# Modulation rows of layers 1 and 2 as two output rows, spread to the partitions by DMA

## What is computed

```python
for layer in (0, 1, 2):                      # layer 0: four experts, gated; layers 1 and 2: one MLP
    mod = silu(c) @ w_ada + b_ada            # [2, 864], one row for each batch element
    sh_msa, sc_msa, g_msa, sh_mlp, sc_mlp, g_mlp = split(mod, 6)
    x = x + g_msa * attention(ln(x) * (1 + sc_msa) + sh_msa)
    x = x + g_mlp * mlp_or_experts(ln(x) * (1 + sc_mlp) + sh_mlp)
x = x + ((x @ U) @ R - x @ U) @ U.T          # U from a QR of P, R from a matrix exponential of c
```

## Time and profile before

| | us |
|---|---|
| three executions: lowest, median, highest | 1153.31, 1158.83, 1162.43 |
| span of the profiled execution, first to last instruction | 1173.7 |
| PE busy, share of the span | 948.9, 81% |
| DVE busy, share of the span | 713.6, 61% |
| ACT busy, share of the span | 412.4, 35% |
| POOL busy, share of the span | 198.5, 17% |
| mean granted clock of TensorE (1 is 2.4 GHz, 0.5 is 1.2 GHz) | 0.638 |

### The profile page before, as it was taken

One profiled execution on the slowest core, in us unless ns is written; L12 is line 12 of the kernel. 1 busy time (PEld: TensorE's weight loads), 2 busy tenths in 40 slices (PEclk: granted clock), 3 DMA queues, 4 the chain that ended last, 5 costly groups with the idle time before them and its releaser, 6 DMA issues.

```text
span 1173.7 us, 12067 instructions
## 1 busy us (share of the span) xinstructions
PE 948.9 (81%) x3791; PEld 513.7 (44%) x3791; DVE 713.6 (61%) x2140; ACT 412.4 (35%) x742; POOL 198.5 (17%) x350
## 2 busy tenths in 40 slices
PE   4666889877898768889877788778887978989847
PEld 1432443335765433357644434535433534335326
DVE  4388767775353887772457767656677365564333
ACT  0302342324341333343424432415332436435412
POOL 5201014010240110042420000311002211012020
PEclk9999755556775655566866555657555656558556
DMA  3000001010111000001110000100000100000000
GB/s 101 13 1 10 16 6 43 1 29 1 29 29 29 17 1 1 1 16 42 34 38 0 1 1 1 29 1 1 1 1 0 30 0 1 1 1 1 6 5 11
DMA packets 22025, 16.01 MB, mean 14 GB/s; under 512 B 6427, under 2 KB 19391, under 8 KB 21962
## 3 DMA queue, kind: packets, MB, share of 16 engines
q1 hardware_dynamic: 21914, 15.22, 4.8%
q10 hardware_dynamic: 48, 0.02, 0.0%
HBM read 14.62 MB, written 0.61 MB: 13 GB/s over the span
## 4 chain that ended last, share of the span: by engine, by line
PE 61%; DVE 29%; issue 4%; ACT 4%; POOL 2%; DMA 0%; DVEq 0%; SPq 0%; ACTq 0%; POOLq 0%
PE o_bank L1289 11%; PE m_bank L1268 11%; DVE row_max L823 7%; PE s_bank L1257 3%; PE m_bank L1466 3%; PE d_bank L1350 3%; PE d_bank L1407 2%; PE d_bank L1409 2%; PE d_bank L1408 2%; PE m_bank L1276 2%; PE d_bank L1306 2%; PE d_bank L1307 2%; PE d_bank L1239 2%; PE d_bank L1392 2%; PE d_bank L1321 2%
## 5 line engine op out<-in xcount | busy, mean ns | idle before, releaser
L663 ACT ACTIVATE probs<-s_bank 128x512 f32<-128x512 f32 x384 | 220.4, 596 | 546.6 <-PE s_bank L1257 544.0
L823 DVE TENSOR_REDUCE row_max<-m_bank 128x1 fp32r<-128x512 f32 x384 | 256.0, 686 | 151.9 <-PE m_bank L1268 147.1
L1268 PE MATMUL m_bank<-k_t,q_t 32*128 32x512 f32 x384 | 216.5, 752 | 61.9 <-DVE q_rows L1079 24.2
L1257 PE MATMUL s_bank<-q_t,k_t 32*128 32x512 f32 x384 | 239.4, 749 | 5.8 <-ACT probs L663 4.9
L1289 PE MATMUL o_bank<-probs,v_aug 128*32 128x512 f32 x768 | 178.2, 1019 | 3.9 <-DVE o_tok L841 3.2
L1268 PEld LDWEIGHTS m_bank<-k_t,q_t 32*128 32x128 f32 x384 | 81.6, 271 | 181.9 <-issue 62.9
L1257 PEld LDWEIGHTS s_bank<-q_t,k_t 32*128 32x128 f32 x384 | 90.6, 272 | 30.9 <-ACT probs L663 16.1
L589 POOL TENSOR_TENSOR h_tok<-h_tok,mod 128x144 f32<-128x144 f32 x48 | 24.0, 499 | 297.3 <-DVE h_tok L882 297.3
L1407 PE MATMUL d_bank<-ff_hi,g_hi 128*128 128x144 f32 x192 | 60.7, 316 | 1.5 <-ACT g_hi L733 1.4
L1409 PE MATMUL d_bank<-ff_lo,g_hi 128*128 128x144 f32 x192 | 60.7, 316 | 0.0
L1408 PE MATMUL d_bank<-ff_hi,g_lo 128*128 128x144 f32 x192 | 60.5, 315 | 0.0
(11 more groups left out here) (232 smaller groups left out, 1639.4 us busy)
## 6 DMA issues: line engine op xcount, KB each, us to landing
raw_a<-in_L_cond_w_dram SPq DMA_DIRECT2D x20, 288.0 KB
raw_a<-in_L_cond_W_fc_dram SPq DMA_DIRECT2D x4, 288.0 KB
w_rows<-in_L_cond_W_dram SPq DMA_DIRECT2D x8, 141.8 KB
raw_d<-in_L_cond_w_dram SPq DMA_DIRECT2D x30, 36.0 KB
raw_a<-in_L_cond_w_dram SPq DMA_DIRECT2D x20, 36.0 KB
x_tok<-in_x_dram SPq DMA_DIRECT2D x2, 288.0 KB, 4.2
out_dram<-moe SPq DMA_DIRECT2D x4, 144.0 KB, 1.9
raw_d<-in_L_cond_w_dram SPq DMA_DIRECT2D x30, 4.0 KB
```

The source lines that it names most:

```text
L663: act.activation(probs[:, n % PROBS, :], s_banks[n % S_BANKS][:, :], ACT.Exp, scale=HD ** -0.5)\
L823: dve.tensor_reduce(row_max[:, grp % 2, t, MAXROW + 32 * j:MAXROW + 32 * j + 1], bk[:, :], AX.X, ALU.max).then_inc(drained, 1)
L1257: pe.matmul(s_banks[n % S_BANKS][:, :], k_t[rows, par, g, kt * P:(kt + 1) * P], q_t[rows, par, g, :], start=True, stop=True).then_inc(s["s ...
L1268: pe.matmul(bk[:, :], q_t[rows, par, g, t * P:(t + 1) * P], k_t[rows, par, g, :], start=True, stop=True).then_inc(s["max_full"], 1)
```

## The change

For layers 1 and 2 the four stages `mods` become two stages `rows(l)` and two stages `spread(l)`. `rows(1)` stands in block 0 where `mods(1, 0)` stood, `rows(2)` in block 2 where `mods(2, 0)` stood; `mods(1, 1)` and `mods(2, 1)` are gone. In `rows(l)` PE multiplies one column of silu(c) for each element, so the product has two output rows, one for each element. ACT copies the two halves out of PSUM into two rows of `g_raw` (borrowed from the MLPs) and stores them to a DRAM scratch tensor. `spread(l)`, at the start of block 1 for layer 1 and of block 3 for layer 2, reads each row back to 128 partitions, by two DMAs that ACT issues. DVE takes no part, but waits for the two transfers before the first normalisation of the layer.

The 1 of the scale now comes out of the product, in layer 0 too: `ada_d` has one more row, 1 for the two scale vectors and 0 for the others, set by POOL at the start, and `c_wide_d` has one more row of ones. So DVE's two instructions for each half in layer 0 become one copy of 432 columns. The first load of `ada_d` waits for that row.

```diff
     if block == 0:
-        out += [("norm", 1, "msa"), ("qkv", 1), ("prep", 1), ("prep", 2), ("mods", 1, 0), ("prep", 3)]
+        out += [("norm", 1, "msa"), ("qkv", 1), ("prep", 1), ("prep", 2), ("rows", 1), ("prep", 3)]
+    if block == 1:
+        out += [("spread", 1)]
     if block >= 1:
         out += after_attention(block - 1)
-    if block == 1:
-        out += [("mods", 1, 1)]
     if block == 2:
-        out += [("mods", 2, 0), ("prep", LAYER_ITEM[2])]
-    if block == 3:
-        out += [("mods", 2, 1)]
+        out += [("rows", 2), ("prep", LAYER_ITEM[2])]
     if 1 <= block < BLOCKS - 1:
         out += [("norm", block + 1, "msa"), ("qkv", block + 1)]
+    if block == 2:
+        out += [("spread", 2)]
...
+        mod_row = g_raw[0:B, :, :].rearrange("p i n -> p (i n)")[:, 0:6 * C]
...
             def load_ada(l):
                 if l:
-                    sp.wait_ge(s["mods_part"], 4 * l)
+                    sp.wait_ge(s["mods_full"], 4 if l == 1 else 6)
+                else:
+                    sp.wait_ge(s["ada_zeroed"], 1)
...
+            link(pool.memset(ada_d[:, :], 0.0))
+            pool.memset(ada_d[:, :].rearrange("p (h v c) -> p h v c", h=2, v=3)[:, :, 1, :], 1.0)\
+                .then_inc(s["ada_zeroed"], 1)
             pool.memset(raw_d[:, :], 0.0).then_inc(s["zeroed"], 1)
...
+            def rows(l):
+                copied = []
+                if seen.n.get("up_full", 0):
+                    act.wait_ge(s["g_lo_ready"], seen.n["up_full"])
+                for half in range(2):
+                    bk, drained, before = ring.take()
+                    act.wait_ge(s["mods_full"], 3 + 2 * l + half)
+                    act.activation(mod_row[:, 3 * C * half:3 * C * (half + 1)], bk[0:B, 0:3 * C], ACT.Copy)\
+                        .then_inc(drained, 1)
+                    copied.append((drained, before + 1))
+                for w in copied:
+                    act.wait_ge(*w)
+                act.dma_start(mod_scratch[l - 1], mod_row[:, :]).then_inc(rows_stored, 16)
+                yield
+
+            def spread(l):
+                act.wait_ge(rows_stored, 16 * l)
+                for b in range(B):
+                    act.dma_start(mod[:, b, l % 2, :, :].rearrange("p v c -> p (v c)"),
+                                  mod_scratch[l - 1][b:b + 1, :].to_broadcast([P, 6 * C])).then_inc(mods_in, 16)
...
-                    dve.tensor_copy(dst[:, 0:3:2, :], src[:, 0:3:2, :]).then_inc(s["mods_part"], 1)
-                    dve.tensor_scalar(dst[:, 1, :], src[:, 1, :], 1.0, None, ALU.add).then_inc(drained, 1)
+                    dve.tensor_copy(mod[:, b, l % 2, 3 * half:3 * half + 3, :],
+                                    bk[:, 0:3 * C].rearrange("p (v c) -> p v c", v=3)).then_inc(drained, 1)
...
             def norm(blk, kind):
                 b = blk % B
+                if kind == "msa" and blk >= B:
+                    dve.wait_ge(mods_in, 16 * B * (blk // B))
...
+            def rows(l):
+                for half in range(2):
+                    bk, _ = take(ring)
+                    pe.wait_ge(ada_in, 48 * (l + 1))
+                    cols = slice(3 * C * half, 3 * C * (half + 1))
+                    pe.matmul(bk[0:B, 0:3 * C], c_wide_a[:, :, 0], ada_a[:, cols], start=True, stop=False)
+                    pe.matmul(bk[0:B, 0:3 * C], c_wide_d[:, :, 0], ada_d[:, cols], start=False, stop=True)\
+                        .then_inc(s["mods_full"], 1)
+                yield
```

More of the change, by code:

```diff
@@ L120 @@
 WOVEN = [st for block in range(BLOCKS) for st in stages(block)]
-BANKS_OF = {"prep": (), "mods": (2,), "norm": (0, 2, 0), "qkv": (2, 2, 2, 2, 2, 2), "proj": (2,), "gate": (1, 0),
+BANKS_OF = {"prep": (), "mods": (2,), "rows": (2,), "spread": (), "norm": (0, 2, 0), "qkv": (2, 2, 2, 2, 2, 2), "proj": (2,), "gate": (1, 0),
             "mlp": (7, 0), "rotate": (2,)}
-ROOM = {"prep": (), "mods": (1,), "norm": (4, 1, 2), "qkv": (2, 2, 2, 2, 2, 2), "proj": (2,), "gate": (2, 1),
+ROOM = {"prep": (), "mods": (1,), "rows": (1,), "spread": (), "norm": (4, 1, 2), "qkv": (2, 2, 2, 2, 2, 2), "proj": (2,), "gate": (2, 1),
         "mlp": (1, 1), "rotate": (1,)}
@@ L258, in build @@
         ada_a = sb("ada_a", [P, 6 * C])
-        ada_d = sb("ada_d", [CR + 1, 6 * C])
+        ada_d = sb("ada_d", [CR + 2, 6 * C])
         c_a = sb("c_a", [P, B])
@@ L265, in build @@
         c_wide_a = sb("c_wide_a", [P, B, P])
-        c_wide_d = sb("c_wide_d", [CR + 1, B, P])
+        c_wide_d = sb("c_wide_d", [CR + 2, B, P])
         raw_a = sb("raw_a", [P, NM])
@@ L337, in build @@
         m_d = sb("m_d", [DW, B, C], F32R)
+        mod_scratch = nc.dram_tensor("mod_scratch", [2, B, 6 * C], F32, kind="Internal").ap()
         v_scratch = nc.dram_tensor("v_scratch", [B * VT, VP], F32, kind="Internal").ap()
@@ L357, in build @@
         scratch_in = sem("scratch_in")
+        rows_stored = sem("rows_stored")
+        mods_in = sem("mods_in")
         skew_in = sem("skew_in")
         y_stored = [sem(f"y_stored{i}") for i in range(2)]
-        names = ("zeroed ident_ready consts_ready weights_ready c_exp c_wide mods_part mods_full xn_ready "
+        names = ("zeroed ident_ready consts_ready weights_ready c_exp c_wide ada_zeroed mods_full xn_ready "
                  "h_tok_ready h_turned h_hi_ready qkv_full qk_normed hi_ready stack_ready stack_turned scores_full probs_ready "
@@ L668, in o_copy @@
                 act.activation(o_t[:, :], o_bank[:, :], ACT.Copy).then_inc(s["o_copied"], 1)
+            def rows(l):
[17 more added lines that the diff above has]
+                                  mod_scratch[l - 1][b:b + 1, :].to_broadcast([P, 6 * C])).then_inc(mods_in, 16)
+                return
+                yield
             def norm(blk, kind):
@@ L747, in solver @@
                     act.activation(q_rows[:, :], bk[0:S, 0:C], ACT.Copy).then_inc(drained, 1)
-            walk = {"norm": norm, "qkv": qkv, "gate": gate, "mlp": mlp}
+            walk = {"rows": rows, "spread": spread, "norm": norm, "qkv": qkv, "gate": gate, "mlp": mlp}
             def side(todo):
@@ L1504, in solver @@
                 last[chain] = ready
-            walk = {"mods": mods, "norm": norm, "qkv": qkv, "proj": proj, "gate": gate, "mlp": mlp,
+            walk = {"mods": mods, "rows": rows, "norm": norm, "qkv": qkv, "proj": proj, "gate": gate, "mlp": mlp,
                     "rotate": rotate}
```

3 lines of the change are left out of this document (removed).

## The result

The changed kernel takes 1162.49 us (median of 20 executions, 1152.71 to 1174.61), beside 1160.7 us for the kernel before in the same comparison (20 executions, 1142.96 to 1169.87). The ratio of the means is 1.0034 [1.0005, 1.0065]: no gain, and at most 0.65% slower. Forecast were 1147 us in 1136 to 1160. The ratios from here on, too, are of the means of all executions, each against before on the same chip, with 95% intervals from resampling and without three lone executions of experiments, at 1213 to 1257 us. Taken only over the executions within 1.5% of each kernel's fastest, a ratio is 0.5 to 1.2% higher (the change 1.0081 [1.0046, 1.0115], e1 1.0017, e8 0.9955), because that drops over half of before's, which spread over 2 to 3%, and few of the others'.

What follows compares the result with a forecast made beforehand. The prediction took PE and DVE to bound the kernel by turns (61% and 29% of the chain). Its terms, -6.4 - 3.5 - 0.4 - 1.3 = -11.6 us from 1158.8, gave 1147 us, range 1136 to 1160.

Steps and rivals of the forecast that it cites:

- Stages dropped, 6.4 + 3.5 us: Dropping modulation stages saves 6.4 us in block 3 (bounds 5.0 to 7.8) and 3.5 in block 1 (2.5 to 4.8).
- The turn of the maxima in block 1, +1.3: Block 1: DVE must wait at L830 for PE's turning of the maxima, 1.12 us and some 0.2 of signals.
- `rows`: Blocks 0 and 2: stationary operand of 2 columns instead of 128 saves 0.6 us a stage (bounds nothing to 2.5).
- DVE's copies, -0.7 in block 0: Blocks 0 and 2: DVE no longer copies the modulation products, saving 0.7 us each.
- ACT's hold-up, +0.9 in block 0: ACT's copy and store issue ahead of the exponential delay block 0's scores by 0.9 us; hidden in block 2.
- `spread`, nothing: Starts of blocks 1 and 3: ACT's two transfers cost nothing, hidden in idle time; without that cover, +0.7 us each.
- the order of slots: Block 3: up to 1.4 us of the saving might go because MLP and normalisation are each one step off.
- within 1%: Outcome class: measured time within 1% (11.6 us) of the kernel before, chance 0.49.
- Given back: Rival: PE only waits for DVE anyway, so just DVE's copies are saved, 2.8 us; 1156 us, chance 0.2.
- ACT pays: Rival: ACT's hold-up falls on the chain in block 2 and at both spreads, +2.3 us; 1150 us, chance 0.1.
- The clock: Rival: MLPs of blocks 1 and 3 change clock steps; worse 1171 us, chance 0.06; better 1136 us, chance 0.1.

Runs made afterwards that it cites:

- e1: The change with an empty slot where each dropped stage stood (blocks 1 and 3), so other stages keep their old steps: 1151.5 us, ratio 0.9930 to before.
- e8: e1 plus GpSimd splitting the next MLP's weights only after the present MLP's last g_lo: 1141.0 us, ratio 0.9833 to before.
- e7: The kernel before with the layer 1 and 2 modulation stages of the second batch element left out, empty slots instead: 1149.5 us, ratio 0.9895.
- e5: The change with block 1's solver parts at steps 21, 23, 26 moved one step on: 1162.4 us, ratio 1.0014 to before.
- e10: The change with the edits of e5 and e6 together: 1151.4 us, ratio 0.9916 to before.
- e13: The change with e6's later weight split and block 1's four MLPs at old steps 20, 22, 24, 26: 1140.4 us, ratio 0.9838 to before.
- e6: The change with GpSimd splitting the next MLP's weights only after the present MLP's last g_lo: 1150.9 us, ratio 0.9910 to before.
- e9: The kernel before with only GpSimd's weight split held until the present MLP's last g_lo: 1150.7 us, ratio 0.9923 to before.

## Why the prediction was wrong

**The sum agrees with the runs at the old places, though not term by term.** *Stages dropped, 6.4 + 3.5 us:* e7 has 12 us less than before by its ratio (8 to 16), and e1, which stands for the whole sum of 11.6, 8 to 10 less. No run separates the two blocks' terms. *The turn of the maxima in block 1, +1.3:* it came onto the chain as said. In the timeline DVE waits for it right behind the solver's step:

```profile
379.15 0.69 DVE L864 SCALAR_TENSOR_TENSOR q_t<-m_bank,q_t 128x512 fp32r<-128x512 f32 x1 [1.27 <-PE m_bank L1309]
```

*`rows`:* PE's stage in block 0 runs from 187.63 to 193.75 in the chain, 6.1 us against the 7.0 of the earlier trace rows. I took 0.6 us for the smaller loads; it is 0.85. By the estimate from the Trainium skill ("TensorE: Matmul & The Clock Gate", "LDWEIGHTS (loading the stationary operand)") it was 0.84, and the trace agrees in that sum, though not in the loads' own times, 311 and 83 ns. *DVE's copies, -0.7 in block 0:* they gave nothing beyond that. From the first product to the row maximum the chain takes 6.9 us, against 7.8 before (to 194.75 in the earlier trace rows), since DVE now waits for the scores that PE does behind the stage. The changed kernel:

```profile
187.63 1.53 PE d_bank L1350 x2
...
194.57 1.29 DVE row_max L857 x2
```

and the start of the stage before:

```profile
186.96 1.74 PE d_bank L1306 x2
```

*ACT's hold-up, +0.9 in block 0:* the second copy and the store lie ahead of the exponential as forecast. ACT's timeline in block 0, and PE's next scores:

```profile
193.78 0.52 ACT L687 ACTIVATE g_raw<-d_bank 2x432 f32<-2x432 f32 x1 [2.54 <-PE d_bank L1351]
194.39 0.46 ACTq L692 DMA_DIRECT2D mod_scratch<-g_raw  x1
194.96 1.09 ACT L672 ACTIVATE probs<-s_bank 128x512 f32<-128x512 f32 x2 [0.65 <-PE s_bank L1290]
...
195.60 0.79 PE L1290 MATMUL s_bank<-q_t,k_t 32*128 32x512 f32 x1 [0.46 <-ACT probs L672]
```

The 0.65 us in brackets hold the issue of the store, 0.46. The scores ended near 194.5, so the exponential came some 0.4 us late, and PE's next scores waited 0.46 for it. It cost nothing on the chain that ended last, which runs through DVE's row maxima there.

*`spread`, nothing:* issued at 235.88 and 4.2 us in landing by the page's DMA issues, where I took 13 for two; DVE needs it only near 370, and no wait for it shows.

```profile
mod<-mod_scratch ACTq DMA_DIRECT2D x4, 432.0 KB, 4.2
```

**The step that failed** is the one on the order of slots. In block 3 I allowed "1.4 us" for it ("the MLP and the normalisation are each one step off"), and only as a bound; in block 1, where three of the four MLPs moved (I counted all four), the sum has no term at all. I asked what a moved MLP does to the clock, and put that at a chance of 0.06, but not what its new neighbours do to it. Measured, the places cost 12 us (e1 against the change, each by its ratio: 0.9930 and 1.0034), as much as the stages gave. The diff could have told where to look, if not how much: the solver's steps are fixed by `QR_PACE`, and the order of the instructions shows them on the MLPs' new steps. That "within 1%" had the largest chance, 0.49, is luck: it came from a forecast on the border of it, not from the places.

**The rivals.** "Given back" had the time nearest to the result (1156), by a mechanism that the runs don't show: e1 keeps the gain. "ACT pays" is 2.3 us above the sum, too little for the result; e1 against e7 leaves room for so much. The clock did not turn against the change: the mean granted clock is 0.631 in its twenty executions and 0.631 in the 29 of before beside e1, and in the traces the MLPs of block 1 take 62.2 us in the change and 67.6 in e1.

**What stays open.** Of the 9 to 10 us that the MLPs' places cost beside the later split, the wait ahead of MLP 0 (3 to 4 us) is read from the trace. How the rest comes about isn't settled. Closing the gaps alone (e5, e10) gave no time, and the stretch of the four MLPs is no shorter in e13's trace than in e6's 70.48 us, though e13 is 10.6 us faster by medians:

```profile
281.58:353.86 72.28, 69.70 (x355) 52.02 (x354) 30.00 (x76) 35.78 (x56) 19.99 (x12) 0.83 0.09 24
```

Each kernel has one trace, and the mean granted clock of the change's twenty executions runs from 0.602 to 0.651, so which clock follows which spacing of the MLPs is not shown.

## What to carry to other kernels

Where slots are spread by weights, taking one out is two edits: the work that goes, and every stage behind and ahead of it that moves. Keep the places with an empty slot first (e1), and only then try moving them. Look at what an MLP or another PE-bound stage covers on DVE at its place, before moving it. And look in the timeline for instructions with two SBUF operands that take several times their usual duration: a GpSimd instruction beside them may be able to start where DVE is idle, which gave some 10 us here, for one wait. With both, the change is worth having: e13 and e8 take 1140.4 and 1141.0 us, 0.9838 and 0.9833 of before by the means; the later split alone (e9) gives 0.9923.

## What the hardware showed that I had not expected

- The stretching is large and sharp: 0.30 to 3.25 us for the same instruction (L1103), ending with POOL's. L1100, which reads one tile as both of its operands, is stretched as well (0.50 here, up to 1.64 in the same trace, 0.30 alone).
- Less idle time of PE among the MLPs went with a lower clock, in one trace each: with 7.5 us less of it (e5), PE's busy time grew by 5.9 us, and the mean granted clock fell from 0.83 to 0.79.
- Executions of one kernel differ by 2.7% on a single core (before: 1141.02 to 1171.85 in 29), and a forecast of 1% can't be read from three of them.
